# The scaled mean of a block: ahead of the exponential in ScalarE's queue, or at the end of its slot

## The reference, cut to what matters

```python
mask = (adj > 0).astype(x.dtype)
deg = jnp.sum(mask, axis=1, keepdims=True)
agg = mask @ x / jnp.maximum(deg, 1.0)                       # the mean over the neighbours
combined = jnp.concatenate([x @ W_self + b_self, agg @ W_nb + b_nb], axis=-1)
x1 = layernorm(x + relu(combined @ W_comb + b_comb))

neib_att = jnp.tanh(neigh @ Wn1 + bn1) @ Wn2 + bn2
value = neigh @ Wv + bv
x_att = jnp.tanh(x1 @ Wx1 + bx1) @ Wx2 + bx2
ws = leaky_relu(x_att @ neib_att.T, 0.01)
ws = softmax(jnp.where(adj > 0, ws, NEG_BIG), axis=1)
out = layernorm(x1 + concatenate([x1 @ Wfx + bfx, ws @ value], axis=1))
```

## Time and profile before

| | us |
|---|---|
| median of 3 runs | 773.29 (772.44 to 774.54) |
| the profiled execution, own time | 773.35 |
| its span, first to last instruction | 771.5 |
| around the span (launch, end) | 1.85 |
| PE busy / PEld busy | 719.8 (93%) / 618.4 (80%) |
| DVE busy / ACT busy / POOL busy | 604.6 (78%) / 585.5 (76%) / 167.7 (22%) |
| chain that ended last | PE 85%, ACT 4%, issue 4%, DVE 4% |
| granted TensorE clock, mean over the span | 0.992 |

### The profile page before, as it was taken

One profiled execution on the slowest core, in us unless ns is written; L12 is line 12 of the kernel. 1 busy time (PEld: TensorE's weight loads), 2 busy tenths in 40 slices (PEclk: granted clock), 3 DMA queues, 4 the chain that ended last, 5 costly groups with the idle time before them and its releaser, 6 DMA issues.

```text
span 771.5 us, 20109 instructions
## 1 busy us (share of the span) xinstructions
PE 719.8 (93%) x7600; PEld 618.4 (80%) x7600; DVE 604.6 (78%) x1343; ACT 585.5 (76%) x1080; POOL 167.7 (22%) x241
## 2 busy tenths in 40 slices
PE   5989989999999999999999999999999999998775
PEld 4556768888888888888888888888888888887554
DVE  4988567888888888888888888888888888877774
ACT  2455267887788788787888788778778788789985
POOL 0010221212222221222222222221222222222201
PEclk9999989999999999999999999999999999999999
DMA  8977995777677777776778677867877777520000
GB/s 268 361 165 162 245 290 145 164 173 178 163 165 181 164 167 183 178 161 174 159 167 179 166 167 175 173 165 178 185 161 171 163 165 179 130 50 9 8 8 14
DMA packets 192560, 124.61 MB, mean 162 GB/s; under 512 B 157776, under 2 KB 176080, under 8 KB 192464
## 3 DMA queue, kind: packets, MB, share of 16 engines
q1 hardware_dynamic: 192020, 123.31, 66.8%
q10 hardware_dynamic: 444, 0.02, 0.0%
HBM read 81.35 MB, written 4.19 MB: 111 GB/s over the span
## 4 chain that ended last, share of the span: by engine, by line
PE 85%; ACT 4%; issue 4%; DVE 4%; DMA 1%; POOL 1%; SPq 0%; ACTq 0%; POOLq 0%; DVEq 0%
PE ps_v L1079 20%; PE ps_t L1066 14%; PE ps_agg L1042 14%; PE ps_agg L1045 14%; PE ps_s L1057 7%; PE ps_agg L1097 3%; PE ps_agg L1100 3%; PE ps_v L964 2%; ACT score L872 2%; PE ps_s L956 2%; PE ps_x L1120 1%; PE ps_x L1117 1%; DVE score L653 1%; PE ps_t L947 1%; PE ps_x L973 1%
## 5 line engine op out<-in xcount | busy, mean ns | idle before, releaser
L1042 PE MATMUL ps_agg<-x,mask_t 128*128 128x257 f16 x1024 | 244.1, 274 | 1.6 <-DMA mask_t<-mask 1.6
L717 DVE TENSOR_TENSOR late<-ps_t,late 128x512 f16<-128x512 f32 x256 | 174.7, 682 | 83.5 <-ACT late L878 83.4
L1045 PE MATMUL ps_agg<-x,mask_t 128*128 128x256 f16 x1024 | 238.2, 274 | 0.0
L1079 PEld LDWEIGHTS ps_v<-v,late 128*128 128x128 f16 x3072 | 190.9, 97 | 50.4 <-DVE late L717 20.5
L865 ACT ACTIVATE score<-ps_s,sc 128x512 f32<-128x512 f32 x256 | 177.5, 693 | 70.3 <-PE ps_s L1057 70.2
L1079 PE MATMUL ps_v<-v,late 128*128 128x128 f16 x3072 | 213.5, 219 | 12.3 <-DVE late L717 8.6
L1066 PE MATMUL ps_t<-ident,score 128*128 128x128 f32 x1024 | 157.9, 277 | 17.7 <-ACT score L872 17.7
L878 ACT CAST late<-ps_t 128x512 f16<-128x512 f32 x256 | 148.9, 582 | 16.5 <-PE ps_t L1066 16.4
L872 ACT ACTIVATE score<-score,exp_bias,sc 128x1024 f32<-128x1024 f32 x128 | 158.4, 1238 | 2.4 <-DVE exp_bias L662 2.4
L653 DVE CUSTOM_DVE_ANT_0 score<-score,mask 128x1024 f32<-128x1024 f32 x128 | 156.0, 1219 | 5.2 <-ACT score L865 5.2
L1066 PEld LDWEIGHTS ps_t<-ident,score 128*128 128x128 f32 x1024 | 108.5, 141 | 24.3 <-ACT score L872 23.7
(11 more groups left out here) (130 smaller groups left out, 764.6 us busy)
## 6 DMA issues: line engine op xcount, KB each, us to landing
adj_sb<-in_adj_dram SPq DMA_DIRECT2D x128, 512.0 KB, 4.2
neigh_sb<-in_L_gnn_neigh_dram SPq DMA_DIRECT2D x8, 512.0 KB, 8.0
score<-in_x_dram SPq DMA_DIRECT2D x8, 512.0 KB, 8.5
x_in<-in_x_dram SPq DMA_DIRECT2D x32, 128.0 KB, 4.0
out_dram<-out_sb SPq DMA_DIRECT2D x32, 128.0 KB, 3.0
mask_t<-mask SPq DMA_TRANSPOSE x128, 3.1
mask<-in_L_gnn_W_comb_dram SPq DMA_DIRECT2D x1, 512.0 KB, 9.1
x_t<-x SPq DMA_TRANSPOSE x32, 4.4
```

Source lines behind the costliest of these rows:

```text
L717: dve.tensor_tensor(p_lo[:, k % 2, :], ps_t[k % 2][:, :], p_hi[:, k % 2, :], ALU.subtract).then_inc(p_lo_made, 1)
L1042: mm = pe.matmul(agg[:, 0:D + 1], mask_t8[:, c, 0, :], x16[:, c, X_HI:X_ONE + 1], start=(c == 0), stop=(c == NC - 1), skip_group_check=True)
L1045: mm = pe.matmul(agg[:, 0:D], mask_t8[:, c, 0, :], x16[:, c, X_LO:X_LO + D], start=False, stop=False, skip_group_check=True)
L1079: mm = pe.matmul(ps_v[:, 0:DV], p[:, k % 2, chunk], v16[:, c, v:v + DV], start=(c == 0 and part == 0), stop=(c == NC - 1 and part == 2))
```

## The change

Two steps are called at another place of their slot. On ACT, `mean_of` no longer stands first in the slot, ahead of the exponential, but after `leaky`, behind the exponential and `p_high`. On DVE, `degrees` is called right after `masked_scores` instead of after `row_max`. No instruction is added or removed, and none has another operand or another semaphore.

```diff
@@ the loop over the slots, VectorE
                 if (d := due(s, SCORE_AT + 2)) and d[1] % 2 == 0:
                     masked_scores(d[0], d[1] // 2)
+                if d := due(s, MEAN_AT, 0):
+                    degrees(d[0])
                 if d := due(s, MEAN_LOW_AT, 0):
                     mean_low(d[0])
...
                 if d := due(s, ROW_MAX_AT, 0):
                     row_max(d[0])
-                if d := due(s, MEAN_AT, 0):
-                    degrees(d[0])
                 if d := due(s, LAYER0_AT, 0):
                     layer0(d[0])
@@ the loop over the slots, ScalarE
                 first_part(s)
-                if d := due(s, MEAN_AT, 0):
-                    mean_of(d[0])
                 if d := due(s, MEAN_SPLIT_AT, 0):
                     mean_high(d[0])
...
                 if d := due(s, SCORE_AT):
                     leaky(*d)
+                if d := due(s, MEAN_AT, 0):
+                    mean_of(d[0])
                 if d := due(s, LAYER1_AT + 1, 0):
                     normalise2(d[0])
```

## The result

| | before | changed |
|---|---|---|
| median | 773.42 us (772.44 to 774.54, 4 runs) | 753.05 us (751.82 to 756.78, 4 runs) |
| the profiled execution | 773.35 | 753.65 |
| its span | 771.5 | 751.8 |

The ratio is 0.9744, 95% interval 0.9707 to 0.9782. The kernel is 20.4 us faster, and the forecast was 753.1. Run again beside the experiments, the same kernel came out at 0.9739 (0.9716 to 0.9762), 752.96 us.

A forecast was written before the change was run, and what follows sets the result against it. PE was taken to bound the middle, idle only at L1066 for the exponential. 27 x 0.72 = 19.44 us plus 0.75 at the end made 20.2 off 773.35, so 753.1 against the median; range 751.2 to 758.8.

The forecast's parts named there:

- What bounds the kernel: Middle blocks: PE sets the pace, 97.6% busy, idle nearly only at L1066, waiting for ACT's exponential.
- The exponential and PE's share of it: Exponential starts 1.31 us earlier; PE's L1066 gains 0.67 plus 0.05, 0.72 us a block; cover 0.64 us.
- The mean's margin: ACT's mean, now behind leaky, ends at 303.80; PE wants it at L1088, 304.40, a margin of 0.60 us.
- DVE: DVE's idle 1.59 us ahead of L717 shrinks by 1.31, since p_high comes earlier; DVE has 18% spare.
- The start and the end: Start: 0.45 us lost in slot 24, 0.38 won at the first exponential, counted 0; last block: 0.75 won.
- the slow stretch: PE at half rate near 110 to 118 us; once more or not at all, 3.4 us at most either way.
- The smaller gain: Rival: bracketed gap is the true size (758.8 us) or mean up to 0.2 us late at PE (758.6); chance 0.11.
- no change: Rival: another releaser keeps the exponential until about 302.36, PE gains nothing, 773 us; chance 0.03.
- the late mean: Rival: PE stalls at L1088 for the mean, slower; 791 us if 2.0 us later than worked out; chance 0.03.

The follow-up runs named there:

- e2: Kernel before, mean still first in ACT's slot, its reciprocal made one slot earlier on DVE: 0.9780, 756.44 us, 20.38 us a block.
- e9: e7 with DVE's row_scale one slot earlier: 0.9749, 754.51 us, 20.31 us a block.
- e3: The change, with the mean one more step back, in the next slot behind x1_high: 0.9751, 753.97 us, 20.27 us a block.
- e4: The change, with the mean in the next slot behind p_high of group 0: 0.9886, 764.66 us, 20.65 us a block.
- e6: The change, with an unused 128x1024 copy on ScalarE ahead of the first exponential of the first 29 blocks: 0.9814, 759.34 us, 20.41 us a block.
- e7: The change, with the mean directly behind the first exponential and an unused 128x1024 ScalarE copy ahead of it: 0.9825, 759.42 us, 20.43 us a block.
- a0: The changed kernel run once more, unaltered, as the yardstick on the experiments' chip: 0.9739, 752.96 us.
- e5: The change, with an unused 128x256 copy on ScalarE ahead of the first exponential of the first 29 blocks: 0.9740, 753.78 us, 20.27 us a block.
- e1: The change, with the mean directly behind the first exponential, ahead of p_high and leaky: 0.9734, 752.64 us.
- e10: e1 with DVE's row_scale one slot earlier, no copy: 0.9713, 751.91 us.

## Why the prediction was right

*What bounds the kernel.* Right. PE set the pace, and the gap ahead of L1066 was the only one of the middle: with it gone, PE is busy for 100% of it.

*The exponential and PE's share of it.* Right to 0.01 us: 0.72 us a block, 20.99 to 20.27. Going by the distances of starts was the choice that mattered, since the gaps in brackets would have given 13.8 instead of 19.4 us. The Trainium skill, "Perfetto Trace Analysis", section "Per-engine timelines", says that a matmul's end is an estimate; the trace agrees, with a gap of 0.51 us that gave 0.67 when it closed. That the wait was the cause and not the place, e2 shows: in the old place, with a shorter wait, nearly all of the time came back. The mean's own 0.38 us alone would have been below the cover. That PE cannot use more of the 1.31 us is shown by e9, where the exponential comes 0.61 us later than with the change and a block takes 20.31 us.

*The mean's margin.* Right: 0.60 worked out, 0.58 measured, and e3, e4 and e6 show it from both sides: a step of 0.26 us back is free, an exponential 0.61 us later just uses it up, and a place behind `p_high` of group 0 costs 0.38.

*DVE.* The wait at L717 fell to 0.31, 1.28 us less for the 1.31 worked out. I wrote that from there on the engines do what they did. They do, but the argument left out the hand-over of `ps_v` (e7, e9). `layer1` ended 0.95 us before the values of group 0 in the change (301.37 and 302.32), and needs 0.12 of that; the margin is 0.8 us there, and 0.5 with the mean, 0.35 us, directly behind the exponential. It changed nothing in the sum, and it is the step that I would add.

*The start and the end.* That 753.1 met 753.05 is in part luck: the four runs of the change lie between 751.8 and 756.8, and two small terms were off to opposite sides. L1066 of the first whole block stood at 135.84 with its wait, so at 135.17 without it; it is now at 136.19. The start so took 1.0 us more and not 0. The two terms that I had, 0.45 lost and 0.38 won, both came. In slot 24 PE lost 0.4:

```profile
97.99 0.38 PE L1057 MATMUL ps_s<-n,stack 96*128 96x512 f16 x1
...
99.51 0.44 PE L1088 MATMUL ps_agg<-ident,mean 128*128 128x128 f32 x2 [0.25 <-ACT mean L855]
```

against 97.42 and 98.54. And at the first exponential of all PE won 0.36: shortly before it the run was 1.03 us behind the kernel before (ACT's L884 at 111.69 and 110.66), and at L1066 behind it 0.67. First row: the change; second: the kernel before:

```profile
114.14 1.12 PE L1066 MATMUL ps_t<-ident,score 128*128 128x128 f32 x4 [0.68 <-ACT score L872]
```
```profile
113.47 1.11 PE L1066 MATMUL ps_t<-ident,score 128*128 128x128 f32 x4 [1.04 <-ACT score L872]
```

The 1.0 us are two things that I hadn't counted. 0.6 are there already at the first mean, at 74.18 us, ahead of any instruction that moved; in the profiled runs of the kernels that have that mean in the same place it stands anywhere from 73.2 to 74.6 (73.59 in the kernel before), so I put this down to the execution and not to the change. And 0.4 are the slow stretch. From 110 to 122 us the mean clock is 0.72 in both, but by the distances between L1042 and L1045 (0.21 or 0.22 us at the low level, 0.11 at the high one) it lasts to about 119.1 us in the change and to 117.7 in the kernel before, so that more of it fell on matmuls. First row: the change; second: the kernel before:

```profile
118.00:120.00 2.00, 2.00 (x15) 1.56 (x14) 0.00 (x0) 2.00 (x4) 0.00 (x0) 0.71 0.67 130
```
```profile
118.00:120.00 2.00, 2.00 (x24) 1.78 (x23) 0.03 (x1) 2.00 (x5) 0.00 (x0) 1.00 0.90 186
```

In the same window it is 0.54 in a0, 0.80 in e5 and 0.89 in e1, so whether the change moved it isn't shown. From L1066 of the last whole block to the end of the span it was 771.5 - 681.50 = 90.0 us, and is 751.8 - 663.13 = 88.7 (663.13 is the mean at 663.41 less the 0.28 by which L1066 is ahead of it). That is 1.3 us, where I had 0.75. ScalarE's part of it is 0.86, since the mean's idle of 0.75 was again an end and a start: by starts it was 0.11 more. Another 0.05 is the group of that last L1066, which had its wait too. The rest of 0.4 us I haven't located. And PE did get the last mean late, as written:

```profile
683.87 0.44 PE L1088 MATMUL ps_agg<-ident,mean 128*128 128x128 f32 x2 [0.76 <-ACT mean L855]
```

So 0.67 (the first wait) + 26 x 0.72 + 1.3 - 1.0 = 19.7 us, which is 773.35 - 753.65. The forecast for this pair of runs was 20.2.

*The rivals.* The smaller gain is out by the 0.67 of the timeline, no change by the exponential that follows its bias, and the late mean by the 0.58 us of margin. e4 shows that the last would have cost 11 to 12 us of the 20 if the mean had been put two steps later.

## What to carry to other kernels

In an in-order queue look for an instruction that waits for something which the ones behind it don't need; if one of those sits on the path, put the waiting one behind it, down to the point where its own reader wants it. Size the gain and the new margin by distances between starts, taken where the same pair of instructions ran without a wait; idle times in brackets came out short by 0.1 to 0.2 us each time. Then list every hand-over that hangs on the moved instruction, through other engines' queues too: here three of them stood within 0.3 us of each other, and the one through VectorE's queue had been overlooked.

## What the runs showed of the hardware

ScalarE's instructions overlap in the records: the mean started 0.58 us after a `leaky` of 0.69 us. A 128x1024 copy of 1.05 us took 0.94 from start to start. An idle time on ScalarE so has to be read as 0.11 us longer than its bracket. The Trainium skill's "Perfetto Trace Analysis", section "Per-engine timelines", says that the recorded window of ScalarE runs until the write is acknowledged. The overlap fits that, but no run here shows what it consists of.

A group of four transpositions that PE has to wait for takes 0.49 or 0.50 us to its successor, and 0.44 or 0.45 where it doesn't; a pair (L1088) 0.27 or 0.28 instead of 0.22. Each wait so cost some 0.05 us more than its own length. The 0.05 came even where the group wasn't late: in e6, e7 and e9 L1073 follows L1086 by the 0.67 us of a start without a wait, 1.38 us behind its exponential, and still takes 0.49. A block that is 0.05 us longer without any wait in the list can be a hand-over that has just used up its margin.

Near the end, where PE waits often, two executions of the same changed kernel differ in the granted clock (first row: the run above; second row: a0):

```profile
694.00:698.00 4.00, 2.25 (x30) 1.71 (x29) 3.83 (x9) 3.48 (x7) 1.59 (x4) 1.00 0.00 0
```
```profile
694.00:698.00 4.00, 2.26 (x23) 1.87 (x21) 3.83 (x11) 3.39 (x7) 1.06 (x4) 0.84 0.00 0
```

With PE busy for 2.25 of 4 us, the clock stayed at 2.4 GHz in the one and went to 1.2 GHz for a part in the other. PE had waited for DVE's L717 just before in both, 1.75 and 1.74 us; the 12 matmuls L1079 behind this wait took 0.84 us in the one and 1.40 in the other. a0's profiled span is 1.0 us longer, and half of that lies here: from L1066 of the last whole block (663.66) to the end it takes 89.1 us instead of 88.7. Of the other half, 0.4 were there at the first mean. With the 2 us of the stretch at the start (e10), such stretches are one source of the spread between runs.
